# Retention scores and q times state: from split products on block-diagonal operands to fp32 matmuls of 64 rows per head

## The reference, cut to what matters

```
q, k = rotary(x @ Wq) * 64**-0.5, rotary(x @ Wk)        # per head h: 64 columns
v    = x @ Wv                                           # per head h: 128 columns
attn = (q_b @ k_b.T) * D                                # within a chunk, D = gamma**(i-j) for i >= j
o    = attn @ v_b + (q_b * cross_q) @ S                 # S is the 64 x 128 state of a head
S    = gC * S + (k_b * cross_k).T @ v_b
o    = rmsnorm(o, gn) * silu(x @ Wg);  x1 = layernorm(x + o @ Wo)
h    = silu(x1 @ wg.T) * (x1 @ wu.T);  out = layernorm(x1 + h @ wd.T)
```

## Time and profile before

| | |
|---|---|
| median of 3 runs | 474.8 us (474.2 to 477.07) |
| the profiled execution | 475.41 us, of which the span from the first to the last instruction is 473.7 us |
| granted TensorE clock, mean | 0.991 |
| TensorE busy | 451.2 us, 95% |
| VectorE busy | 338.4 us, 71% |
| ScalarE busy | 316.5 us, 67% |
| GpSimd busy | 234.7 us, 50% |

### The profile page before, as it was taken

One profiled execution on the slowest core, in us unless ns is written; L12 is line 12 of the kernel. 1 busy time (PEld: TensorE's weight loads), 2 busy tenths in 40 slices (PEclk: granted clock), 3 DMA queues, 4 the chain that ended last, 5 costly groups with the idle time before them and its releaser, 6 DMA issues.

```text
span 473.7 us, 10345 instructions
## 1 busy us (share of the span) xinstructions
PE 451.2 (95%) x3174; PEld 414.4 (87%) x3174; DVE 338.4 (71%) x836; ACT 316.5 (67%) x922; POOL 234.7 (50%) x382
## 2 busy tenths in 40 slices
PE   7878699999999999999999999999999999999994
PEld 4767588999999999999999999999999999998994
DVE  5799546667787667688776667886676688766764
ACT  4788747666677567666676666676676757766452
POOL 3654144443666354554654435663544546542564
PEclk9999979999999999999999999999999999999999
DMA  7820101001010110101011010100101010000001
GB/s 242 287 71 1 47 1 46 2 13 55 13 42 16 35 33 11 55 11 38 23 27 33 11 55 11 55 11 22 33 26 40 11 35 11 30 8 11 12 25 45
DMA packets 15933, 18.45 MB, mean 39 GB/s; under 512 B 1440, under 2 KB 13728, under 8 KB 15904
## 3 DMA queue, kind: packets, MB, share of 16 engines
q1 hardware_dynamic: 15904, 18.09, 12.0%
HBM read 13.89 MB, written 4.19 MB: 38 GB/s over the span
## 4 chain that ended last, share of the span: by engine, by line
PE 88%; DVE 3%; issue 3%; ACT 2%; DMA 1%; POOL 1%; SPq 1%; POOLq 0%; DVEq 0%; ACTq 0%
PE b_rows L354 46%; PE b_ffn L354 18%; PE b_o L436 5%; PE b_score L354 5%; PE b_turn L466 3%; PE b_o L354 3%; PE b_state L354 3%; PE b_turn L368 3%; DMA wf_int<-in_w_proj 1%; PE b_turn L416 1%; ACT sq L730 1%; DVE z L1043 0%; DVE wf_int L955 0%; ACT state_hi L740 0%; SPq L271 0%
## 5 line engine op out<-in xcount | busy, mean ns | idle before, releaser
L354 PE MATMUL b_ffn<-x1T_hi,wf_hi 128*128 128x256 f32 x384 | 96.0, 286 | 3.9 <-issue 3.9
L354 PE MATMUL b_ffn<-x1T_lo,wf_hi 128*128 128x256 f32 x384 | 95.3, 284 | 0.0
L1220 POOL TENSOR_TENSOR h_lo<-wf_int,h_hi 128x256 fp32r<-128x256 f32 x96 | 69.7, 739 | 45.3 <-ACT h_hi L766 45.3
L354 PE MATMUL b_rows<-wp_hi,xT_hi 128*128 128x512 f32 x192 | 79.6, 415 | 4.0 <-DVE z L1043 1.5
L354 PEld LDWEIGHTS b_ffn<-x1T_hi,wf_hi 128*128 128x128 f32 x384 | 73.4, 191 | 5.4 <-issue 4.1
L354 PE MATMUL b_rows<-wp_lo,xT_hi 128*128 128x512 f32 x192 | 76.8, 400 | 0.0
L354 PE MATMUL b_rows<-wp_hi,xT_lo 128*128 128x512 f32 x192 | 76.5, 399 | 0.0
L1237 POOL TENSOR_TENSOR ms_eps<-ms,eps 128x4 f32<-128x4 f32 x32 | 7.0, 220 | 139.5 <-ACT sq L730 139.5
L354 PEld LDWEIGHTS b_ffn<-x1T_lo,wf_hi 128*128 128x128 f32 x384 | 73.5, 191 | 1.4
L1007 DVE TENSOR_TENSOR yT_lo<-b_turn,yT_hi 128x512 fp32r<-128x512 f32 x32 | 22.1, 690 | 47.8 <-ACT yT_hi L718 47.8
L955 DVE TENSOR_TENSOR wf_int<-b_ffn,wf_int 128x256 f32<-128x256 f32 x96 | 38.3, 421 | 21.7 <-ACT wf_int L755 20.9
(11 more groups left out here) (101 smaller groups left out, 1320.2 us busy)
## 6 DMA issues: line engine op xcount, KB each, us to landing
xT_raw<-in_xT SPq DMA_DIRECT2D x16, 256.0 KB, 3.0
x_sb<-in_x SPq DMA_DIRECT2D x16, 256.0 KB, 2.7
out<-wf_int SPq DMA_DIRECT2D x32, 128.0 KB, 1.7
wf_int<-in_w_ffn SPq DMA_DIRECT2D x6, 384.0 KB, 7.2
wf_int<-in_w_proj SPq DMA_DIRECT2D x6, 256.0 KB, 5.0
rope_sb<-in_rope SPq DMA_DIRECT2D x4, 256.0 KB, 7.0
wo_raw<-in_w_o SPq DMA_DIRECT2D x1, 512.0 KB, 7.5
gn_sb<-in_gn SPq DMA_DIRECT2D x1, 0.5 KB, 6.7
```

What stands on the lines that cost most here:

```text
L354: mm = pe.matmul(dst, a, b, start=(i == 0 and j == 0 and not begun), stop=(i == n - 1 and j == len(passes) - 1 and not more), skip_group_c ...
L1220: pool.tensor_tensor(h_lo[:, ring, hb], h_full[:, u], h_hi[:, ring, hb].bitcast(F32), ALU.subtract).then_inc(h_split[j], 1)
```

## The change

`qkT_hi`, `qkT_lo` and the two diagonals are replaced by one fp32 tile `qkT`, the state's two parts by one fp32 tile `state`. ScalarE makes each with plain copies; VectorE's `split_qk` and `split_state` and the four copies that cleared the diagonals go. `score` is one fp32 matmul a head of 64 rows (rows 0 to 63 for heads 0 and 2, rows 64 to 127 for heads 1 and 3), 128 columns each; q times state likewise, all four heads first and the four products with v after them. The banks `b_score` and `b_o` are replaced by two banks `b_head`: one holds scores and o of heads 0 and 2, the other those of heads 1 and 3. So `score` now also waits for y of the tile before, and `mask` is two instructions. VectorE's `rotate_parts` is cut in two around the aggregation of the second layernorm.

```diff
-        b_score = bank("b_score")
-        b_o = bank("b_o")
+        b_head = [bank("b_head0"), bank("b_head1")]
...
+        def half(h):
+            return slice((h % 2) * DK, (h % 2 + 1) * DK)
+        def scores_of(h):
+            return b_head[h % 2][:, (h // 2) * P:(h // 2 + 1) * P]
+        def o_of(h):
+            return b_head[h % 2][:, 256 + (h // 2) * DV:256 + (h // 2 + 1) * DV]
...
 # TensorE, score
-                    pe.wait_ge(qdiag_high, n + 1)
-                    pe.wait_ge(qdiag_low, n + 1)
+                    pe.wait_ge(qkT_kept, n + 1)
                     if exists(n - 1):
                         pe.wait_ge(masked, n)
-                    for pr in range(2):
-                        diag = [w[:, pr].rearrange("p a b -> p (a b)") for w in (qdiag_hi, qdiag_lo)]
-                        mm = split_product(b_score[:, pr * 2 * P:(pr + 1) * 2 * P],
-                                           [(qkT_hi[:, 2 + pr], qkT_lo[:, 2 + pr])], [diag])
+                        pe.wait_ge(y_ready, n)
+                    for h in range(H):
+                        mm = pe.matmul(scores_of(h), qkT[half(h), 2 + h // 2], qkT[half(h), h // 2],
+                                       start=True, stop=True)
...
 # TensorE, retain
-                if exists(n - 1):
-                    pe.wait_ge(y_ready, n)
                 if tn > 0:
-                    pe.wait_ge(state_split, states_to(qn, tn - 1))
-                for pr in range(2):
-                    if tn > 0:
-                        mov = [w[:, pr].rearrange("p a b -> p (a b)") for w in (state_hi, state_lo)]
-                        split_product(b_o[:, pr * 2 * DV:(pr + 1) * 2 * DV], [(qkT_hi[:, pr], qkT_lo[:, pr])],
-                                      [mov], begun=pr > 0, more=True)
-                    for h in (2 * pr, 2 * pr + 1):
-                        mm = pe.matmul(b_o[:, h * DV:(h + 1) * DV], attn[:, h, :],
...
+                    pe.wait_ge(state_kept, states_to(qn, tn - 1))
+                    for h in range(H):
+                        pe.matmul(o_of(h), qkT[half(h), h // 2], state[half(h), h // 2],
+                                  start=h < 2, stop=False, skip_group_check=True)
+                for h in range(H):
+                    mm = pe.matmul(o_of(h), attn[:, h, :], v_sb[:, tn % 2, h * DV:(h + 1) * DV],
+                                   start=(tn == 0 and h < 2), stop=h >= 2, skip_group_check=True)
...
 # ScalarE
+                    act.copy(qkT[:], b_turn[:].rearrange("p (b n) -> p b n", b=4)).then_inc(qkT_kept, 1)
...
-                        last = act.copy(state_hi[rows, :, a, :], b_state[rows].rearrange(
+                        last = act.copy(state[rows], b_state[rows].rearrange(
...
 # VectorE, mask
-                    dve.tensor_tensor(attn[:], b_score[:].rearrange("p (a b) -> p a b", a=H),
-                                      causal[:].unsqueeze(1).broadcast_to((P, H, P)), ALU.mult).then_inc(masked, 1)
+                    by_half = attn[:].rearrange("p (c a) n -> p a c n", a=2)
+                    for a in range(2):
+                        last = dve.tensor_tensor(by_half[:, a], b_head[a][:, 0:256].rearrange("p (c n) -> p c n", c=2),
+                                                 causal[:].unsqueeze(1).broadcast_to((P, 2, P)), ALU.mult)
+                    last.then_inc(masked, 1)
...
 # VectorE, slot
-                split_qk(s, q, t)
+                rotate_cos(s, q, t)
                 moments_2(n6 - 1, t7, waited=True)
-                rotate_parts(s, q, t)
+                rotate_sin(s, q, t)
...
                 if is_slot(s, NT - 1):
                     hidden(s, t, 0)
-                    split_qk(NT, NSEQ, 0)
-                    split_state(s, q, t)
                     gated_output(s, q, t)
```

More of the change, by code:

```diff
@@ L129, in build_block @@
         qk = sb("qk", [P, 2, 512])
[L131 to L135, removed]
+        qkT = sb("qkT", [P, 4, P])
         v_sb = sb("v_sb", [P, 2, V])
@@ L140, in build_block @@
         attn = sb("attn", [P, H, P])
-        state_hi = sb("state_hi", [P, 2, 2, DV], F32R)
-        state_lo = sb("state_lo", [P, 2, 2, DV], F32R)
+        state = sb("state", [P, 2, DV])
         sq = sb("sq", [P, P])
@@ L185, in build_block @@
         x_in = [sem(f"x_in{r}") for r in range(2)]
-        consts, cleared = sem("consts"), sem("cleared")
+        consts = sem("consts")
         wp_high, wp_split = sem("wp_high"), sem("wp_split")
@@ L195, in build_block @@
         rot_parts, rotated = sem("rot_parts"), sem("rotated")
-        qkT_done, qkT_high, qkT_split = sem("qkT_done"), sem("qkT_high"), sem("qkT_split")
-        qdiag_high, qdiag_low = sem("qdiag_high"), sem("qdiag_low")
+        qkT_done, qkT_kept = sem("qkT_done"), sem("qkT_kept")
         v_copied, g_gated = sem("v_copied"), sem("g_gated")
@@ L201, in build_block @@
         o_done, state_done = sem("o_done"), sem("state_done")
-        state_high, state_split = sem("state_high"), sem("state_split")
+        state_kept = sem("state_kept")
         squared, ms_ready, rms_ready, y_ready = sem("squared"), sem("ms_ready"), sem("rms_ready"), sem("y_ready")
@@ L342, in _ @@
             row_stages = [(0, rot_parts), (0, v_copied), (0, g_gated), (2, z1_ready), (DOWN_LAG, z2_ready)]
-            turn_stages = [(1, qkT_split), (X1T_LAG, x1T_split), (2, yT_split)]
+            turn_stages = [(1, qkT_kept), (X1T_LAG, x1T_split), (2, yT_split)]
             def split_product(dst, stat, mov, begun=False, more=False):
@@ L446, in update_state @@
                     if tn == 0 and exists(n - 2):
-                        pe.wait_ge(state_split, states_to(qn, tn) - 1)
+                        pe.wait_ge(state_kept, states_to(qn, tn) - 1)
                     pe.wait_ge(kv_split, states_to(qn, tn))
@@ L560, in last_slot @@
                 down(s, q, t, wide, (1, 2))
-                turn_y(NT, NSEQ, 0, free=(qkT_split, NT))
+                turn_y(NT, NSEQ, 0, free=(qkT_kept, NT))
                 retain(NT, NSEQ, 0)
@@ L636, in split_xT, with keep_qk @@
                 act.copy(xT_hi[:, ring, :, at:at + P], xT_raw[:, ring, :, at:at + P]).then_inc(xT_high, 1)
-            def split_qk(s, q, t, between=None):
+            def keep_qk(s, q, t):
                 n = s - 1
[L641 to L660, removed]
+                if exists(n):
+                    act.wait_ge(qkT_done, n + 1)
+                    if exists(n - 1):
+                        act.wait_ge(o_done, n)
+                    act.copy(qkT[:], b_turn[:].rearrange("p (b n) -> p b n", b=4)).then_inc(qkT_kept, 1)
             def keep_x1(s, q, t):
@@ L666, in keep_x1 @@
                     act.wait_ge(x1_ready, n + 1)
+                    if is_slot(s, FFN_LAG):
+                        act.wait_ge(low_squared, NFP - 2)
                     if exists(n - 4):
@@ L729, in mean_squares, with keep_state @@
                             act.wait_ge(squared, 4 * n + h)
-                        act.activation(sq[:], b_o[:, h * DV:(h + 1) * DV], ACT.Square, scale=float(DV) ** -0.5,
+                        act.activation(sq[:], o_of(h), ACT.Square, scale=float(DV) ** -0.5,
                                        accum_out=ms[:, tn % 2, h:h + 1]).then_inc(squared, 1)
-            def split_state(s, q, t):
+            def keep_state(s, q, t):
                 qn, tn = back(q, t, 1)
@@ L739, in split_state @@
                         rows = slice(a * DK, (a + 1) * DK)
-                        last = act.copy(state_hi[rows, :, a, :], b_state[rows].rearrange(
+                        last = act.copy(state[rows], b_state[rows].rearrange(
                             "p (c n) -> p c n", c=2)[:, :, a * DV:(a + 1) * DV])
-                    last.then_inc(state_high, 1)
+                    last.then_inc(state_kept, 1)
             def gate(s, t, j):
@@ L789, in slot @@
             def slot(s, q, t, ahead):
-                if not is_slot(s, NT):
-                    split_qk(s, q, t)
+                keep_qk(s, q, t)
                 if sparse(s - 1):
@@ L810, in slot @@
                 mean_squares(s, q, t)
-                split_state(s, q, t)
+                keep_state(s, q, t)
                 if is_slot(s, 2):
@@ L819, in slot @@
                 if is_slot(s, NT - 1):
-                    split_qk(NT, NSEQ, 0, lambda: split_h(s, t, 0))
+                    keep_qk(NT, NSEQ, 0)
+                    split_h(s, t, 0)
                     gate(s, t, 1)
@@ L897, in tell_wide @@
                 dve.tensor_copy(wide_flag[:], wide_parts[:]).then_inc(wide_known, 1)
[L899 to L907, removed]
             def moments_2(n, tn, waited=False):
@@ L915, in moments_2, with rotate_cos @@
                     dve.bn_aggr(mv2[:, tn % 2], st2[:, tn % 2]).then_inc(z2_moments, 1)
-            def rotate_parts(s, q, t):
+            def rotate_cos(s, q, t):
+                n7 = s - DOWN_LAG - 1
                 if exists(s):
                     dve.wait_ge(qk_done, s + 1)
```

(9 more changed lines are left out.)

3 lines of the change are left out of this document (removed).

## The result

The changed kernel takes 481.04 us (median of 4 runs, 480.78 to 481.86) against 475.86 for the kernel before beside it: a ratio of 1.0113, 95% interval 1.0081 to 1.0144. It is slower by 1.1%; 466.5 was forecast, in a range of 459 to 486. The profiled execution took 480.91 us, its span is 479.1 us against 473.7.

What follows compares the result with a forecast made beforehand. TensorE's stream was taken to bound the kernel (busy 95%). Bursts at -8.7 us, with start and ends about +0.2, gave -8.5: 466.9 from the profiled 475.4, 466.3 from the median; forecast 466.5, range 459 to 486.

Steps and rivals of the forecast that it cites:

- What bounds the kernel: Whole span: TensorE busy 95%; in the middle only time taken off its stream shortens the result.
- record count: TensorE's matmul records: were to go from 3174 to 3286.
- part 4: VectorE and ScalarE in the loop: the work they lose is covered by TensorE's stream, worth 0.
- Part 3: Changes between 128 and 64 rows, two a burst, 112 in all: cost taken as 0; other bound 0.16 to 0.35 us.
- Parts 1 and 2: Scores (32 tiles) and q times state (24 tiles): fp32 passes replace split products, 56 x -0.155 = -8.7 us.
- 5T: A burst's eight passes take five pass lengths of 0.111 us, 0.555 us, if starts stay in program order.
- 4T: A burst's eight passes take four pass lengths, 0.445 us, if the halves run fully side by side.
- full overlap: Rival for the bursts: both halves run side by side throughout, -14.8 us, 460.8 us in all; chance 0.11.
- emptying: Rival: array emptied at each change of rows, 17.9 to 39 us more, 484.8 to 506 us; chance 0.15.
- Part 5: Added wait for y before the scores: 0 in the loop; at the start slots 3 and 4 wait, together +1.5 us.
- Part 6: The ends: sum over the low weights no longer waits for ScalarE, -0.5 us; last tile's scores, -0.75 us.
- The halves taking turns: Rival for the bursts: only one half streams at a time, eight pass lengths, 485.7 us in all; chance 0.16.

Runs made afterwards that it cites:

- e1_rows128: The changed kernel with every fp32 matmul of scores and q times state on all 128 rows, values not the reference's: 483.6 us (one run).
- e8_half_by_half: The changed kernel with the heads of each burst in the order 0, 2, 1, 3: 481.87 us (one run).
- e2_one_half: The changed kernel with all four heads on rows 0 to 63, values not the reference's: 507.77 us (one run).
- e3_one_burst: The changed kernel with q times state issued directly behind the scores: 482.78 us, ratio to the kernel before 1.0144.
- e7_all: The changed kernel with one burst per tile, x1's transposes before the projection to g, and y at the end of its slot from the start: 466.12 us, ratio 0.9798.
- e9_before_x1_first: The kernel before with only the transposes of x1 moved ahead of the projection to g: 472.78 us, ratio 0.9949.

## Why the prediction was wrong, point by point

- **What bounds the kernel, record count, part 4** (the other engines' relief is worth nothing in the loop): right. 89 us less busy time on VectorE and ScalarE moved nothing there.
- **Part 3, the boundary**, is the step that failed. I took 0, from a change of number format that costs nothing, against a bound of 0.16 to 0.35. It is 0.20 each, 0.40 a burst, 56 x 0.40 = +22.4 us by the chain. Its own sign showed in the trace: at both changes the weight load starts only with its matmul, and the first pass of a burst is listed longer. The nearest row was near in kind, not in cause: it changes the format and keeps the rows, and e1_rows128 shows exactly that this is free. The rule of the Trainium skill ("TensorEngine Tiling (Array Packing)", Key Properties), that a change of tiling mode drains TensorE, agrees with these traces in that each change of rows costs time, and they add how much: 0.20 us. How much of it is emptying and how much the weight load that no longer goes ahead, no run separates. The bound built from rows, a matmul's 0.28 less the 0.12 between starts, was 0.16, close to the 0.20.
- **Parts 1 and 2, the bursts**: also wrong, the other way. I took 5T on an argument from program order; it is 4T (0.445), 56 x 0.11 = -6.2 us more. e8_half_by_half refutes the argument. What the Trainium skill says of row groups ("TensorE: Matmul & The Clock Gate", Part 3), that loads and matmuls in different ones overlap with starts some 4 ns apart, agrees with the 7 ns here. That matmuls stay in program order, which the same part says, does not agree with e8_half_by_half: with both heads of one half first, eight passes still took four lengths.
- The two errors together are +16.2 us on my -8.7: +7.5 by the chain, +7.0 by the slots, a tile with a state 0.25 us longer instead of 0.31 shorter. Parts 5 and 6 came to -1.6 us by the spans (5.4 less 7.0), where I had +0.2. I had full overlap and emptying as two rivals and gave neither the other's condition; together they would have given 460.8 + 17.9 = 478.7 with my own 0.16, and the measured time is 481.0. They are not exclusive, and a chance for both at once was missing.
- **Part 5**: in the loop right, no wait for y. In the start three waits of 4.6 us instead of 2.3 in two; I had given slot 2 none, and it has 1.17. Moving y takes all but 0.3 of it out and was worth 3.9 us.
- **Part 6**: the scores of the last tile don't wait any more, as forecast; the end came 0.6 us nearer although the last slots hold four bursts (+0.5), so -1.1 where I had -0.75. The sum over the weights still waited 0.4 us for ScalarE, not nothing.
- The halves taking turns: excluded by e2_one_half, where a burst that really runs one pass after another takes 1.08 us instead of 0.65.

## What to carry to other kernels

A matmul of fewer rows is priced with its neighbours: the gain is one length per pair on two halves, the price is paid per change of rows, and the half of it that is paid on leaving lands on the next instruction's line. Collect all matmuls of one tile shape in one burst and count the changes before counting the passes; with two bursts a tile this form lost 1.1%; with one burst and the moves of x1 and y it won 2%, of which the move of x1 alone gives the kernel before 0.5%. One burst without these moves won nothing (e3_one_burst). And when an instruction is moved away from between two others, look at which transfer between engines it had been covering. Before the starts of two profiles are compared, compare their granted clocks stretch by stretch: here they differed in the first 70 us by up to a third (from 10 to 20 us 1.00 in e7_all, 0.66 in e9_before_x1_first), and in the loop not at all.

## What the runs showed of the hardware that I had not expected

- Going from 128-row matmuls to 64-row ones costs 0.19 to 0.20 us and going back 0.20 (0.15 when two transposes come next, in e7_all), the same with one half in use (e2_one_half) or both. At such a change the weight load starts together with its matmul; with 128 rows on both sides of the same place it started 0.23 us ahead (e1_rows128).
- Two fp32 matmuls of 64 rows by 128 columns on different halves run fully side by side: 16 passes in one burst took 0.65 + 0.45 us (e3_one_burst), of which 0.20 is the entry, 0.056 a pass against 0.111 on 128 rows or on one half.
- They do so even when the program puts both heads of one half first (e8_half_by_half, 0.65 us a burst).
